# One core: the written order of a gated attention and ternary FFN kernel laid out anew, for all five engines

## The chip, the cores and the metric

The kernel runs on one core of a Trainium2 chip. The metric is the device time of one execution in microseconds (us). A core has a matmul engine (TensorE, here PE), VectorE (DVE), ScalarE (ACT), GpSimd (POOL) and SyncE (SP), which here only issues DMA transfers. SBUF is the on-chip working memory of 128 partitions, PSUM the memory that PE writes. About 1% of the time (14 us) is what a measurement of this kernel can tell from no change.

## The reference, cut to what matters

```python
def _L0_xattn_ref(q, k, v, Wq, Wk, Wv, Wo, bo, g):       # 8 heads of 64, DIM 128, b = 16, n = 1024
    qh = softmax(Wq q, over the 64 of a head) * 64 ** -0.5
    kh = softmax(Wk k, over n)
    vh = Wv v
    context = einsum('bhdn,bhen->bhde', kh, vh)
    out = einsum('bhde,bhdn->bhen', context, qh)
    out = Wo out + bo
    return out / norm(out over DIM) * g * sqrt(DIM)

def _bitlinear(x, w):
    scale = mean(abs(w))
    return x @ (round(clip(w / (scale + 1e-5), -1, 1)) * scale).T

x = x + tanh(g_xattn) * _L0_xattn_ref(layernorm(x), ctx, ctx, ...)      # x, ctx: (16, 128, 1024)
h = layernorm(x)
x = x + tanh(g_ffn) * _bitlinear(_bitlinear(h, w_gate) * _bitlinear(h, w_up), w_down)    # I = 2752
```

All values are float32 at the borders. Inside, the kernel splits most operands into a high and a low 16-bit part (`_hi`, `_lo`) and adds three products; ternary weights are kept as fp8.

## The kernel before, in words

The 16 batch elements go through the attention one by one (index i), and through the FFN in 8 groups of two (index g). Each piece of work is a *step* with a name and indices, and most steps take one to three instructions on one engine:

- Context side of i: `cabs`, `csum`, `cscale`, `c_hi`, `c_lo` scale and split the context rows; `kt(i,p)` (PE, L856) makes the keys of a pair of heads, `kmax` (DVE, L1496), `kexp` (ACT, L1224) the softmax; `kf_hi` (ACT), `kf_lo` (DVE, L1518, the subtraction L1358) split them; `turn_c`, `turn_k` are DMA transposes from SP; `ctxk` multiplies. `mprod`, `mev`, `mabs`, `msum`, `mscale`, `m_hi`, `m_lo` make the 128x512 matrix that the queries are multiplied with.
- Query side of i: `ln1` (DVE, L1491), `rstd1` and `q32` (POOL, L1756, L1769), `q_hi` (ACT), `q_lo` (POOL, L1776, the subtraction L1767); `qt(i,u)` (PE, L901), `qmax`, `qsub` (DVE, L1583, L1593), `qexp` (ACT, L1262), `qsum` (DVE, L1596, a reduce L1599 and a reciprocal L1601), `qnorm` (POOL, L1781), `qf_hi` (ACT), `qf_lo` (DVE, L1603, the operation L1361), `turn_q` (SP). For i = 0 and 1 the transposes are matmuls (`tr`, `ktr`, `zt`) in place of DMAs.
- Joining: `outp(i,hf)` (PE, L971), `yev` (ACT), `ss` (PE, L993), `ssg` (DVE, L1608), `rs` (POOL, L1787, the power L1790), `R` (PE, L1001), `x2m` (DVE, L1614), `x2a` (POOL, L1793), `ln2` (DVE), `rstd2` (POOL, L1762, the power L1764), `z` (DVE, L1635). Then z is split and transposed: by `zt` (PE, L878), `zt_hi` (ACT, L1170), `zt_lo` (DVE, L1646, L1358) for i = 0 and 1, by `z_hi`, `z_lo`, `turn_z` later.
- Weights: `wload` (SP) loads tiles of 128x1024 float32 into 13 slots; `wsum` (ACT and DVE) sums the absolute values; `wpart` (DVE, L1414), `wtotal` (PE, L964) and `wscale` (DVE, L1420) give the scale; the tiles are loaded once more, and `wquant` (POOL, L1745, the instruction L1754) and `wsign` (ACT, L1198, L1216) round them to fp8. Matrices 0 and 1 (gate and up) go first, matrix 2 (down) after them.
- FFN of group 0: `gu(0,j,s)` (PE, L1010, the matmul L1029), 22 chunks j of gate and up, then `gcopy` (ACT, L1327), `gmul` (DVE, L1704, the instruction L1709), `i_hi` (ACT, L1338), `i_lo` (DVE, L1713, the subtraction L1358 of 128x256), and `down(0,k,part)` (PE, L1080, L1113). The chunks use two PSUM banks in turn: `gu` of chunk j waits for `gmul` of j - 2. The first down product waits for `i_hi` and `i_lo` of chunks 0 to 20.
- FFN of groups 1 to 7: 20 of the 22 chunks are computed by seven products in place of eight. `form` (DVE and POOL, L1660 and L1813, 128x2048 fp8) makes sums and differences of the weights, `store_form` writes them to HBM, and for each group `load_form` (SP) brings them back; `product` (PE, L1042, the matmul L1064), `evict` (ACT, and DVE L1695), `pair_mul` (POOL, L1832), `pair_hi`, `pair_lo`, then `down` again.
- `reload`, `finish` (DVE, L1727) and `st_out` write the result.

Each engine runs its own instructions strictly in the order in which they are written. That order comes from one table, `WHEN`, which gives each step of each kind its place in one list of some 3,700 steps. `every_step()` names the steps, and each engine's `program` walks the list and emits the steps that it has. Between engines semaphores are waited for: a step that comes up before its input is there holds all that stands behind it on its engine.

```python
def program(steps):
    for _, kind, args in ORDER:
        if kind in steps:
            steps[kind](*args)
```

PSUM banks are handed on in the order in which the steps are written. `kt`, `qt`, `zt` and others share the pair PROJ (n even) and the pair TR (n odd, from i = 2 on): a PE step waits until the last user of the pair has been read, for `kt` by `kexp`, for `qt` by `qsub`, for `zt` by `zt_lo`. SP issues the DMAs of weights, transposes, forms and results, ACT those of x and the context.

Of the kernel before, what the change touches and what calls it, by code (L numbers as in the profile page):

```python
# [107 lines left out]
    "kexp": [27, 30, 99, 127, 169, 194, 209, 271, 357, 377, 399, 431, 468, 645, 648, 684, 768, 868, 922, 983, 1151, 1162,
        1199, 1222, 1248, 1346, 1355, 1377, 1422, 1547, 1558, 1571, 1760, 1767, 1800, 1827, 1941, 1965, 1982, 1989,
        2179, 2189, 2224, 2253, 2375, 2396, 2399, 2411, 2601, 2611, 2646, 2675, 2797, 2818, 2821, 2833, 3023, 3033,  # L110
        3068, 3097, 3214, 3228, 3239, 3249],
    "ktr": [66, 83, 112, 131, 187, 225, 261, 291],
    "k_f": [75, 87, 119, 135, 190, 231, 270, 296],
    "kf_hi": [365, 412, 445, 482, 531, 650, 693, 788, 851, 925, 989, 1017, 1158, 1192, 1228, 1251, 1285, 1350, 1374, 1403,
        1440, 1551, 1582, 1612, 1773, 1805, 1830, 1862, 1953, 1975, 1996, 2040, 2194, 2220, 2248, 2276, 2379, 2402,
        2419, 2462, 2616, 2642, 2670, 2698, 2801, 2824, 2841, 2884, 3038, 3064, 3092, 3120, 3218, 3237, 3252, 3304],
    "kf_lo": [374, 416, 451, 488, 541, 653, 725, 795, 858, 959, 994, 1025, 1163, 1198, 1233, 1255, 1308, 1354, 1378, 1409,
        1444, 1555, 1586, 1618, 1780, 1812, 1838, 1865, 1957, 1981, 2000, 2046, 2202, 2228, 2255, 2282, 2381, 2405,
        2425, 2468, 2624, 2650, 2677, 2704, 2803, 2827, 2847, 2890, 3046, 3072, 3099, 3126, 3220, 3240, 3256, 3320],
# [1758 lines left out]
```

## Time and profile before

| | us |
|---|---|
| median of 3 runs | 1412.72 |
| lowest and highest | 1410.63, 1420.97 |
| the profiled execution, its own time | 1418.48 |
| its span, first to last instruction | 1416.7 |
| PE busy | 1323.1 (93%) |
| VectorE busy | 1014.4 (72%) |
| ScalarE busy | 637.1 (45%) |
| GpSimd busy | 610.9 (43%) |
| mean granted TensorE clock | 0.97 |

Times in the rows count from the first instruction; the profiled execution is the span and 1.8 us around it. A row of busy times gives, for a stretch, each engine's busy microseconds with the number of instructions, the mean granted clock of TensorE (1 is full speed, 2.4 GHz), the DMA engines' share and rate. "A <- B" in a row of waits is what A's engine waited for.

### The profile page before, as it was taken

To read this page: it belongs to the slowest core of one execution; us is meant where nothing else is said; L and a number is where in the kernel's file an instruction comes from. 1 tells how busy PE (TensorE), PEld (TensorE's weight loads), DVE (VectorE), ACT (ScalarE), POOL (GpSimd) and SP (SyncE) were. 2 spreads that over 40 slices of the span, in tenths; PEclk is the share of its full clock that TensorE was granted. 3 is DMA by queue.
4 is the path that set the end of the run, shared out by engine and by line. 5 is a ranking of instruction groups with operands and counts; after the bars stand their busy time and mean duration, and the time that the engine had idled before them with its cause. 6 is when DMAs were issued, how large, how long until landed. Compare 5 with 4: busy or idle time off the path is not lost.

```text
span 1416.7 us, 31262 instructions
## 1 busy us (share of the span) xinstructions
PE 1323.1 (93%) x12888; PEld 970.6 (69%) x12888; DVE 1014.4 (72%) x1337; ACT 637.1 (45%) x866; POOL 610.9 (43%) x369
## 2 busy tenths in 40 slices
PE   4787698878989999999999999999999999999999
PEld 2554385663568955887578856987498757994994
DVE  6877499997878967687768785888568865842330
ACT  4677875554345444444434534454335433330220
POOL 0169755897533435354424460446234432231120
PEclk8898799999999999999999999999999999999999
DMA  9949998996898688778858896779767975664421
GB/s 358 408 152 332 287 268 258 248 226 154 209 206 203 157 172 181 166 180 177 207 129 182 179 193 150 182 176 202 186 155 175 191 168 124 166 154 111 137 79 45
DMA packets 410621, 270.30 MB, mean 191 GB/s; under 512 B 330032, under 2 KB 346800, under 8 KB 410480
## 3 DMA queue, kind: packets, MB, share of 16 engines
q1 hardware_dynamic: 403568, 243.13, 69.9%
q10 hardware_dynamic: 6912, 25.17, 5.7%
q8 instruction: 103, 1.69, 0.5%
q14 instruction: 38, 0.31, 0.1%
HBM read 161.55 MB, written 25.95 MB: 132 GB/s over the span
## 4 chain that ended last, share of the span: by engine, by line
PE 59%; DVE 1%; issue 0%; DMA 0%; POOL 0%; ACT 0%; SPq 0%; DVEq 0%; ACTq 0%; POOLq 0%
PE ps L1064 25%; PE ps L1113 16%; PE ps L817 5%; PE ps L818 5%; PE ps L819 5%; PE ps L1029 2%; PE ps L997 1%; PE ps L1005 1%; DMA kT<-k 0%; PE ps L834 0%; POOL q_raw L1773 0%; DVE k_unit L1474 0%; DVE w_gu L1695 0%; POOL w_gu L1832 0%; DVE q_stat L1599 0%
## 5 line engine op out<-in xcount | busy, mean ns | idle before, releaser
L1113 PE MATMUL ps<-w_dn,inter_buf 128*128 128x512 fp8e4 x1376 | 309.6, 380 | 4.4 <-ACT w_dn L1216 3.7
L1113 PEld LDWEIGHTS ps<-w_dn,inter_buf 128*128 128x128 f16 x1376 | 134.7, 99 | 160.4 <-ACT w_dn L1216 4.4
L1784 POOL TENSOR_TENSOR qs<-qs,q_stat 128x1024 f32<-128x1024 f32 x64 | 133.0, 2079 | 191.3 <-DVE q_stat L1601 190.7
L1064 PE MATMUL ps<-w_gu 128*128 128x128 f16 x3392 | 204.4, 219 | 3.1 <-issue 2.1
L1064 PEld LDWEIGHTS ps<-w_gu 128*128 128x128 fp8e4 x3392 | 195.3, 98 | 10.2 <-issue 3.9
L1832 POOL TENSOR_TENSOR w_gu<-w_gu 128x512 f32<-128x512 f32 x70 | 104.0, 1486 | 211.4 <-DVE w_gu L1695 147.3
L1064 PE MATMUL ps<-zT,w_gu 128*128 128x128 f16 x2528 | 155.3, 220 | 0.0
L1064 PEld LDWEIGHTS ps<-zT,w_gu 128*128 128x128 fp8e4 x2528 | 147.3, 99 | 6.0 <-issue 3.6
L1695 DVE SCALAR_TENSOR_TENSOR w_gu<-ps,w_gu 128x512 f32<-128x512 f32 x140 | 95.7, 684 | 73.9 <-PE ps L1064 72.8
L1029 PE MATMUL ps<-zT,w_gu 128*128 128x256 f16 x1024 | 119.2, 276 | 6.1 <-DVE gate L1709 6.1
L1029 PEld LDWEIGHTS ps<-zT,w_gu 128*128 128x128 fp8e4 x1024 | 101.5, 100 | 23.7 <-DVE gate L1709 7.2
L1500 DVE TENSOR_REDUCE kmx<-ps 128x1 f32<-128x1024 f32 x64 | 77.9, 1217 | 51.3 <-PE ps L819 39.3
L1790 POOL TENSOR_TENSOR rsv<-ssv,cst 128x4 f32<-128x4 f32 x32 | 42.5, 1329 | 157.3 <-DVE ssv L1612 157.3
L1125 ACT ACTIVATE w_gu<-ps 128x512 f32<-128x512 f32 x105 | 62.4, 595 | 99.2 <-PE ps L1064 99.2
L1583 DVE TENSOR_REDUCE q_stat<-ps 128x16 f32<-128x1024 f32 x64 | 77.9, 1218 | 33.4 <-PE ps L819 28.8
L1125 ACT ACTIVATE p<-qs 128x1024 f16<-128x1024 f32 x56 | 59.0, 1053 | 83.2 <-POOL qs L1784 53.0
L1361 DVE SCALAR_TENSOR_TENSOR p<-qs,p 128x1024 f16<-128x1024 f32 x56 | 79.6, 1421 | 18.4 <-ACT p L1125 18.3
L1230 ACT ACTIVATE ek<-ps,kbias,k_unit 128x1024 f32<-128x1024 f32 x56 | 67.3, 1201 | 56.0 <-DVE kbias L1509 55.7
L1268 ACT ACTIVATE qs<-qs,l_used 128x1024 f32<-128x1024 f32 x56 | 64.2, 1146 | 61.6 <-DVE qs L1593 52.9
L1125 ACT ACTIVATE inter_buf<-w_gu 128x512 f16<-128x512 f32 x70 | 43.8, 626 | 105.9 <-POOL w_gu L1832 105.7
L1797 POOL TENSOR_TENSOR xb<-xb,ysq 128x512 f32<-128x512 f32 x32 | 48.4, 1512 | 88.3 <-DVE ysq L1619 88.3
L1358 DVE TENSOR_TENSOR k<-ek,k 128x1024 f16<-128x1024 f32 x56 | 75.9, 1356 | 12.6 <-ACT k L1125 12.4
(192 smaller groups left out, 2660.3 us busy)
## 6 DMA issues: line engine op xcount, KB each, us to landing
w_gu<-forms SPq DMA_DIRECT2D x185, 256.0 KB, 3.1
ct_raw<-forms SPq DMA_DIRECT2D x60, 256.0 KB, 3.0
w_dn<-in_down_w SPq DMA_DIRECT2D x19, 512.0 KB, 5.0
xb<-in_x ACTq DMA_DIRECT2D x16, 512.0 KB, 6.0
x_dram<-xb SPq DMA_DIRECT2D x16, 512.0 KB, 4.1
fin<-x_dram SPq DMA_DIRECT2D x32, 256.0 KB, 2.8
out<-fin SPq DMA_DIRECT2D x32, 256.0 KB, 2.7
inter_buf<-in_up_w SPq DMA_DIRECT2D x15, 512.0 KB, 10.1
```

The lines of the kernel that those rows point to most:

```text
L817: nc.tensor.matmul(out_ap, a_h, b_h, start=start, stop=False)
L1029: last = nc.tensor.matmul(ps[:, rest_bank(g, j), s * T:s * T + T], w_gu[:, w, k, :], zT[:, h, k, :], start=(k == 0 and h == 0), stop=(k == ...
L1064: last = nc.tensor.matmul(o, form[:, c, k, :], moving(q, h, k), start=(fresh and c == 0 and k == 0 and h == 0), stop=(k == 3 and h == 1), ...
L1113: mm = nc.tensor.matmul(ps[:, down_bank(g, k), :], inter_of(g, j, u % 2, b), w_dn[:, j, hf * 512:hf * 512 + 512], start=(u == 0), stop=(u ...
L1125: return nc.scalar.activation(out_ap, in_ap, ACT.Copy, scale=scale)
L1358: return nc.vector.tensor_tensor(out_ap, a, b_ap, ALU.subtract)
L1361: return nc.vector.scalar_tensor_tensor(out=out_ap, in0=a, scalar=by, in1=b_ap, op0=ALU.mult, op1=ALU.subtract)
L1500: nc.vector.tensor_reduce(kmx[:, col], pair(proj_bank(i, p)), AX_X, ALU.max, negate=True).then_inc(k_maxed, 1)
L1583: nc.vector.tensor_reduce(q_stat[:, u % 2, 0, :], per_head(pair(proj_bank(i, u))), AX_X, ALU.max).then_inc(q_max, 1)
L1695: nc.vector.scalar_tensor_tensor(out=out, in0=ps[:, slot_bank(g, s, q), :], scalar=B_SCALE, in1=add, op0=ALU.mult, op1=ALU.add).then_inc(e ...
L1784: nc.gpsimd.tensor_tensor(v, v, q_stat[:, u % 2, 1, :].unsqueeze(2).broadcast_to([P, 2 * HEADS, DH]), ALU.mult).then_inc(q_prob, 1)
L1832: nc.gpsimd.tensor_tensor(v[:, :, 0, :], v[:, :, 0, :], v[:, :, 1, :], ALU.mult).then_inc(pair_muled, 1)
```

## The change

The table `WHEN` holds other places for the same steps. No step, instruction, wait, tile or transfer is added or taken away, and `every_step`, `program` and the steps' own code are the same; only the order within each engine's list changes. By engine: SP has 635 steps of which 232 stand at another place, by 11 places at most; PE 924, 478, 30; ACT 775, 455, 24; DVE 1023, 626, 39; POOL 363, 165, 7. The diff, cut (the numbers are places in the one list; the k-th number of a kind belongs to its k-th step):

```diff
@@ -89,244 +89,244 @@
...
 WHEN = {
...
-    "qnorm": [96, 134, 148, 186, 265, 311, 338, 367, 516, 533, 563, 623, 680, 798, 830, 928, 957, 1018, 1048, 1072, 1136,
...
+    "qnorm": [96, 134, 148, 186, 271, 313, 366, 377, 495, 522, 588, 631, 709, 795, 833, 950, 977, 1022, 1047, 1074, 1147,
...
-    "rs": [200, 273, 385, 433, 704, 850, 979, 1035, 1145, 1227, 1425, 1468, 1573, 1630, 1761, 1810, 1961, 2012, 2183,
...
+    "rs": [200, 267, 404, 436, 718, 849, 984, 1037, 1163, 1232, 1419, 1470, 1579, 1654, 1751, 1812, 1951, 2012, 2176,
...
-    "x2a": [211, 297, 398, 441, 737, 877, 992, 1050, 1180, 1252, 1435, 1475, 1598, 1649, 1779, 1832, 1983, 2039, 2197,
...
+    "x2a": [211, 290, 414, 444, 734, 884, 1000, 1053, 1181, 1250, 1427, 1481, 1605, 1662, 1777, 1835, 1970, 2039, 2193,
...
-    "rstd2": [318, 453, 912, 1060, 1268, 1483, 1658, 1849, 2070, 2305, 2492, 2727, 2914, 3148, 3302, 3494],
+    "rstd2": [310, 455, 909, 1063, 1261, 1491, 1678, 1888, 2070, 2300, 2492, 2722, 2914, 3144, 3302, 3494],
-    "zt": [362, 471],
+    "zt": [379, 486],
-    "zt_lo": [371, 477],
+    "zt_lo": [387, 505],
-    "ln1": [22, 48, 210, 491, 665, 956, 1089, 1329, 1525, 1728, 1963, 2154, 2330, 2576, 2752, 2998],
+    "ln1": [22, 50, 210, 494, 678, 957, 1090, 1307, 1506, 1750, 1975, 2154, 2392, 2576, 2814, 2998],
-    "qt": [74, 79, 106, 155, 213, 220, 282, 324, 479, 483, 539, 592, 651, 718, 773, 874, 926, 997, 1016, 1049, 1095,
-        1181, 1257, 1263, 1310, 1434, 1462, 1487, 1577, 1632, 1673, 1698, 1808, 1844, 1882, 1930, 2015, 2048, 2083,
...
+    "qt": [74, 79, 106, 155, 213, 220, 327, 338, 474, 476, 539, 583, 662, 713, 785, 906, 932, 997, 1020, 1052, 1089,
+        1179, 1251, 1260, 1321, 1434, 1454, 1480, 1546, 1614, 1677, 1704, 1820, 1843, 1865, 1922, 2014, 2048, 2083,
...
-    "qsum": [91, 128, 143, 182, 235, 305, 325, 358, 509, 528, 558, 619, 671, 791, 820, 923, 950, 1013, 1043, 1067, 1132,
...
+    "qsum": [91, 128, 143, 182, 235, 289, 358, 368, 490, 517, 579, 627, 694, 788, 824, 945, 973, 1018, 1041, 1070, 1142,
...
-    "gu": [487, 493, 500, 506, 513, 521, 527, 534, 542, 549, 562, 571, 576, 582, 596, 609, 617, 624, 638, 644, 647,
...
+    "gu": [509, 514, 523, 528, 533, 545, 552, 559, 564, 569, 592, 596, 603, 608, 617, 629, 641, 648, 671, 675, 677,
...
-    "i_lo": [520, 536, 548, 561, 573, 597, 612, 631, 681, 714, 716, 747, 782, 789, 824, 826, 846, 865, 879, 917, 929,
-        941, 1140, 1153, 1565, 1584, 2006, 2014, 2428, 2436, 2850, 2858, 3267, 3274, 3550, 3556],
+    "i_lo": [531, 553, 565, 582, 600, 635, 645, 649, 665, 720, 722, 755, 781, 798, 829, 832, 855, 859, 887, 899, 933,
+        934, 1137, 1141, 1564, 1589, 1997, 2015, 2416, 2440, 2838, 2862, 3257, 3275, 3550, 3556],
-    "form": [277, 568, 575, 588, 649, 687, 691, 708, 740, 775, 784, 819, 810, 839, 866, 884, 871, 967, 982, 995],
+    "form": [283, 566, 573, 595, 618, 669, 674, 681, 736, 766, 775, 818, 817, 864, 874, 890, 935, 982, 989, 1005],
-    "wtotal": [219, 224, 712],
+    "wtotal": [219, 224, 705],
-    "wscale": [223, 228, 717],
+    "wscale": [223, 228, 716],
-    "wquant": [227, 232, 237, 241, 246, 250, 253, 257, 260, 279, 283, 289, 293, 303, 307, 321, 326, 329, 334, 342, 347,
-        352, 356, 360, 364, 373, 376, 381, 390, 394, 401, 403, 406, 411, 417, 422, 426, 430, 436, 450, 455, 461,
...
+    "wquant": [227, 232, 237, 241, 246, 250, 253, 259, 262, 280, 286, 294, 299, 303, 307, 321, 324, 328, 332, 337, 342,
+        344, 349, 354, 359, 363, 373, 382, 385, 389, 392, 397, 399, 406, 410, 420, 425, 428, 432, 447, 451, 458,
...
-    "turn_c": [314, 565, 870, 1099, 1294, 1449, 1726, 1899, 2143, 2363, 2565, 2785, 2987, 3203],
+    "turn_c": [316, 585, 854, 1099, 1294, 1463, 1656, 1874, 2144, 2355, 2566, 2777, 2988, 3199],
-    "turn_k": [380, 420, 460, 492, 564, 659, 731, 801, 872, 966, 999, 1030, 1167, 1204, 1237, 1262, 1314, 1359, 1385, 1415,
...
+    "turn_k": [370, 419, 460, 491, 584, 658, 729, 805, 856, 920, 980, 1003, 1158, 1201, 1239, 1269, 1302, 1380, 1414, 1438,
...
```

Read out of the table, the stretches of the engines' lists that are spoken of below (last index 0 left out, a span of tiles written once):

```
POOL before: qnorm(1,1) rstd2(0) wquant x4 qnorm(1,2) wquant x6 qnorm(1,3) wquant x3 rs(1,0) wquant x2 x2a(1,0)
             wquant x8 rs(1,1) wquant(0,19) x2a(1,1) wquant(1,19) rstd2(1) wquant x4 q_lo(2)
POOL after:  qnorm(1,1) wquant x11 qnorm(1,2) wquant(0,13) qnorm(1,3) wquant x6 rs(1,0) wquant x2 x2a(1,0)
             wquant x4 rs(1,1) x2a(1,1) wquant(1,19) wquant(0,20) rstd2(1) wquant x3 q_lo(2)
PE before:   kt(3,0) zt(1) qt(2,0) qt(2,1) gu(0,0,0) gu(0,0,1)
PE after:    kt(3,0) qt(2,0) qt(2,1) zt(1) kt(3,1) gu(0,0,0) gu(0,0,1)
DVE before:  z(1) kmax(3,0) wsum(2,0) zt_lo(1) qmax(2,0) kf_lo(2,3) ln1(3) qsub(2,0) qmax(2,1) gmul(0,0)
             qsum(2,0) qsub(2,1) i_lo(0,0) gmul(0,1)
DVE after:   z(1) kmax(3,0) wsum(2,0) qmax(2,0) qsub(2,0) qmax(2,1) kf_lo(2,3) qsum(2,0) ln1(3) qsub(2,1)
             zt_lo(1) qf_lo(2,0) qsum(2,1) cabs(4) gmul(0,0) kf_lo(3,0) i_lo(0,0) wsum(2,3) wsum(2,6) gmul(0,1)
POOL before: rstd1(4) q32(4) qnorm(3,0) form(1,2) rs(2,0) form(1,5) wquant(2,0)
POOL after:  form(1,2) form(1,5) rstd1(4) q32(4) qnorm(3,0) rs(2,0) wquant(2,0)
DVE before:  gmul(0,10) qf_lo(2,3) i_lo(0,9) i_lo(0,10) wscale(2)
DVE after:   gmul(0,10) wscale(2) i_lo(0,9) i_lo(0,10)
DVE before:  gmul(0,18) form(4,4) i_lo(0,18) cc_lo(3) qmax(3,3) ln2(2) qf_lo(3,2) qsub(3,3) gmul(0,19) gmul(0,20)
             kmax(4,2) mev(3) i_lo(0,19) mabs(3) qsum(3,3) mscale(3) i_lo(0,20)
DVE after:   gmul(0,18) kmax(4,1) qf_lo(3,2) i_lo(0,18) gmul(0,19) ln2(2) mev(3) i_lo(0,19) mabs(3) gmul(0,20)
             gmul(0,21) kf_lo(4,1) qmax(3,3) kmax(4,2) z(2) qsub(3,3) i_lo(0,20) i_lo(0,21) form(4,4)
```

## Rows read from the trace of the kernel before

**Rows 1.** Busy time of each engine by stretch: us, busy, (instructions), clock, DMA.
```profile
0.00:75.00 75.00, 48.03 (x160) 29.95 (x161) 57.15 (x85) 40.59 (x67) 7.17 (x12) 0.82 0.99 385
75.00:180.00 105.00, 78.19 (x341) 49.03 (x340) 69.39 (x98) 83.83 (x98) 81.23 (x63) 0.85 0.79 252
180.00:323.00 143.00, 118.36 (x898) 90.73 (x895) 139.36 (x152) 86.15 (x135) 103.27 (x46) 0.94 0.95 252
323.00:450.00 127.00, 116.77 (x982) 77.32 (x983) 97.43 (x126) 54.88 (x69) 60.57 (x35) 0.96 0.86 187
450.00:1417.00 967.00, 961.78 (x10516) 723.59 (x10513) 651.12 (x880) 371.66 (x499) 358.63 (x215) 1.00 0.70 160
```

**Rows 2.** PE's waits from 450 on: total, times, longest.
```profile
PE ps L1064 <- DVE w_gu L1695: 0.9, 2, 0.5
```

**Rows 3.** PE's waits from 180 to 323.
```profile
PE ps L817 <- DVE qs L1593: 6.2, 2, 3.6
```

**Rows 4.** DVE by group and shape, 180 to 330: busy, mean ns, idle.
```profile
L1358 DVE TENSOR_TENSOR inter_buf<-gate,inter_buf 128x256 f16<-128x256 f32 x21 | 28.5, 1366 | 0.0
L1361 DVE SCALAR_TENSOR_TENSOR p<-qs,p 128x1024 f16<-128x1024 f32 x7 | 14.3, 2046 | 0.8 <-ACT p L1125 0.8
...
L1667 DVE TENSOR_TENSOR ct_raw<-w_gu 128x2048 fp8e4<-128x2048 fp8e4 x4 | 10.2, 2544 | 0.0
...
L1709 DVE SCALAR_TENSOR_TENSOR gate<-ps,gate 128x256 f32<-128x256 f32 x21 | 8.5, 411 | 0.1
```

**Rows 5.** Timeline 203.5 to 209, all engines: start, us, instruction, [idle before].
```profile
203.70 3.95 POOL L1818 TENSOR_TENSOR w_gu<-w_gu 128x2048 fp8e4<-128x2048 fp8e4 x1 [2.23 <-DVE w_gu L1672]
...
204.48 1.20 DVE L1411 TENSOR_REDUCE absum<-w_dn 128x1 f32<-128x1024 f32 x1
...
205.60 3.13 DVE L1361 SCALAR_TENSOR_TENSOR p<-qs,p 128x1024 f16<-128x1024 f32 x1
```

**Rows 6.** Timeline of POOL, 80 to 170.
```profile
117.84 1.90 POOL L1784 TENSOR_TENSOR qs<-qs,q_stat 128x1024 f32<-128x1024 f32 x1 [1.44 <-DVE q_stat L1601]
...
139.61 1.01 POOL L1790 TENSOR_TENSOR rsv<-ssv,cst 128x4 f32<-128x4 f32 x1
...
156.37 1.01 POOL L1790 TENSOR_TENSOR rsv<-ssv,cst 128x4 f32<-128x4 f32 x1
...
159.43 1.26 POOL L1797 TENSOR_TENSOR xb<-xb,ysq 128x512 f32<-128x512 f32 x1 [0.94 <-DVE ysq L1619]
...
162.53 1.47 POOL L1764 TENSOR_TENSOR mv<-mv,cst 128x1 f32<-128x1 f32 x1 [0.74 <-DVE mv L1489]
...
167.93 2.13 POOL L1767 TENSOR_TENSOR qn<-q_raw,qn 128x1024 f16<-128x1024 f32 x1
```

**Rows 7.** Timeline of DVE, 160 to 182.
```profile
171.53 1.22 DVE L1358 TENSOR_TENSOR zT<-ps,zT 128x1024 f16<-128x1024 f32 x1 [2.87 <-ACT zT L1125]
175.66 1.23 DVE L1583 TENSOR_REDUCE q_stat<-ps 128x16 f32<-128x1024 f32 x1 [2.90 <-PE ps L819]
```

**Rows 8.** Timeline of PE, 140 to 182.
```profile
146.50 5.37 PE L985 MATMUL ps<-eT,m 128*128 128x512 f32 x8 [1.11 <-ACT eT L1125]
...
168.50 1.07 PE L884 MATMUL ps<-ident,ysq 128*128 128x128 f32 x8 [3.54 <-ACT ek L1230]
172.90 0.58 PE L817 MATMUL ps<-wq,qn 128*128 128x512 f16 x1 [3.33 <-DVE zT L1358]
...
177.59 4.64 PE L1029 MATMUL ps<-zT,w_gu 128*128 128x256 f16 x41
```

**Rows 9.** Timeline of POOL, 218 to 260.
```profile
234.01 1.00 POOL L1760 TENSOR_TENSOR mv<-mv,cst 128x1 f32<-128x1 f32 x1 [13.86 <-DVE mv L1489]
...
254.02 4.34 POOL L1754 TENSOR_SCALAR w_dn<-w_dn,wthr 128x1024 f32<-128x1024 f32 x3 [1.25 <-DVE wthr L1429]
```

**Rows 10.** PE's waits from 323 to 450.
```profile
PE ps L1113 <- ACT w_dn L1216: 3.7, 3, 2.7
PE ps L1005 <- issue: 3.3, 1, 3.3
```

More of the change, by code:

```diff
@@ L108 @@
[L108 to L119, printed above, removed]
@@ new lines @@
+    "kexp": [27, 29, 99, 127, 169, 194, 209, 273, 322, 380, 405, 437, 471, 570, 654, 679, 767, 882, 929, 974, 1139, 1152,
+        1187, 1224, 1247, 1355, 1365, 1400, 1426, 1528, 1537, 1576, 1733, 1782, 1795, 1808, 1946, 1962, 1965, 1998,
+        2180, 2187, 2218, 2249, 2375, 2382, 2400, 2421, 2602, 2609, 2640, 2671, 2797, 2804, 2822, 2843, 3024, 3031,
+        3062, 3093, 3217, 3224, 3239, 3258],
+    "ktr": [66, 83, 112, 131, 187, 225, 265, 281],
+    "k_f": [75, 87, 119, 135, 190, 231, 270, 298],
@@ new lines @@
+    "mabs": [636, 903, 1088, 1371, 1519, 1687, 1901, 2102, 2328, 2524, 2750, 2946, 3172, 3373],
+    "msum": [639, 937, 1092, 1376, 1534, 1690, 1908, 2108, 2333, 2530, 2755, 2952, 3177, 3375],
+    "mscale": [78, 107, 640, 949, 1103, 1381, 1542, 1699, 1911, 2112, 2338, 2534, 2760, 2956, 3182, 3378],
+    "m_hi": [643, 951, 1110, 1384, 1549, 1702, 1912, 2123, 2344, 2545, 2766, 2967, 3188, 3383],
+    "m_lo": [647, 954, 1113, 1388, 1553, 1709, 1917, 2126, 2348, 2548, 2770, 2970, 3192, 3386],
+    "ld_xq": [1, 163, 473, 622, 928, 1064, 1278, 1492, 1722, 1944, 2138, 2362, 2560, 2784, 2982],
[3 rows of a table added]
@@ new lines @@
+    "q_hi": [467, 594, 915, 1055, 1267, 1483, 1710, 1928, 2125, 2352, 2547, 2774, 2969, 3196],
+    "q_lo": [469, 607, 921, 1058, 1270, 1486, 1714, 1935, 2129, 2353, 2551, 2775, 2973, 3197],
[4 rows of a table added]
+    "qmax": [81, 103, 113, 165, 221, 249, 333, 346, 479, 485, 548, 593, 672, 732, 794, 919, 952, 1002, 1025, 1056, 1106,
+        1188, 1259, 1272, 1325, 1437, 1460, 1484, 1555, 1620, 1695, 1718, 1823, 1860, 1871, 1937, 2019, 2054, 2088,
+        2132, 2236, 2265, 2282, 2354, 2437, 2476, 2510, 2554, 2658, 2687, 2704, 2776, 2859, 2898, 2932, 2976, 3080,
+        3109, 3126, 3198, 3282, 3332, 3343, 3407],
@@ new lines @@
+    "tr": [102, 146, 193, 206, 314, 334, 384, 396],
+    "e_f": [109, 151, 197, 215, 319, 339, 391, 402],
+    "qf_hi": [503, 567, 626, 706, 761, 827, 877, 985, 1007, 1040, 1069, 1166, 1204, 1234, 1304, 1429, 1445, 1473, 1497,
+        1600, 1629, 1660, 1729, 1766, 1846, 1885, 1923, 1971, 2032, 2085, 2133, 2191, 2263, 2298, 2321, 2398, 2454,
+        2507, 2555, 2613, 2685, 2720, 2743, 2820, 2876, 2929, 2977, 3035, 3107, 3142, 3165, 3233, 3299, 3348, 3374,
+        3431],
+    "qf_lo": [508, 571, 630, 708, 773, 836, 881, 987, 1012, 1046, 1080, 1169, 1211, 1236, 1313, 1430, 1449, 1475, 1500,
+        1604, 1637, 1663, 1738, 1771, 1850, 1897, 1930, 1973, 2038, 2089, 2143, 2197, 2268, 2305, 2326, 2401, 2460,
+        2511, 2565, 2619, 2690, 2727, 2748, 2823, 2882, 2933, 2987, 3041, 3112, 3149, 3170, 3238, 3307, 3354, 3380,
```

197 lines of the change are left out of this document (91 added, 106 removed), and 166 rows, old and new, of the table WHEN.

## The prediction

> **What bounds the kernel now.** I read the busy times by stretch first [rows 1]. TensorE (PE) is busy 1323.1 of 1416.7 us, so it stands idle for 93.6 us, and nearly all of that lies early: 27.0 us before 75, 26.8 us from 75 to 180, 24.6 us from 180 to 323 (the time at which the first down product begins), 10.2 us from 323 to 450. From 450 to 1416.7 it is idle for 5 us of 967, most of it after the last matmul; its largest wait there comes to 0.9 us in two pieces [rows 2]. The change leaves the number of matmuls alone. So what it can bring lies in the idle 88.6 us before 450, and after 450 it can only lose.
>
> The second reading is what fills the stretch 180 to 323: VectorE (DVE) is busy 139.4 of 143 us there [rows 1], and PE's largest wait names it (6.2 us for L1593's subtraction, which gives a bank back) [rows 3]. DVE is the bound of that stretch. It isn't all work. The `i_lo` subtraction of 128x256 takes 1366 ns on average, 21 times, while its neighbour L1709 of the same size takes 411 [rows 4]. One overlap shows how: a `qf_lo` (L1361, 128x1024) starts at 205.60, while GpSimd (POOL) is in a `form` from 203.70 to 207.65, and takes 3.13 us; the same operation has a mean of 2046 ns in this stretch. A reduce of as many elements that starts 1.1 us earlier, under the same POOL instruction, takes its usual 1.20 [rows 5]. DVE operations with two inputs in SBUF are held until POOL's instruction is over. The excess is 21 x (1.37 - 0.41) = 20 us on `i_lo` and 7 x (2.05 - 1.2) = 6 us on `qf_lo`, 26 us of 139.
>
> **The change part by part.** Nothing is added or removed; each engine gets its own instructions in another order, and SP its DMA issues. I walk the places where the order moves something past the chain that feeds PE, in time.
>
> (1) 0 to 75: only neighbours among the small scale steps change places. Cost 0.
>
> (2) POOL from 88 to 170. The chain to the first `gu` goes through POOL's queue: rs(1,1) at 156.37, x2a(1,1) at 159.43, rstd2(1) at 162.53, and q_lo(2) from 167.93 to 170.06, with `wquant` tiles between [rows 6]. Waits of 0.94 and 0.74 us stand there, because x2a and rstd2 come up in the queue before DVE has delivered. The new list has the same steps ahead of q_lo(2). rs(1,1) has one `wquant` more ahead, x2a(1,1) none more, rstd2 one more. So POOL does its tile before it needs DVE and the wait of 0.74 goes; an earlier wait of 1.44 us of qnorm(1,1) for DVE's row sums [rows 6] should go too, as qsum(1,1) moves ahead of qsub(1,2). Against it stands that x2a(1,1) now follows rs(1,1) with no tile between: its wait grows from 0.94 to about 2. Net -1 to -2; I take -1.5. Bounds: 0 and -4 (all of POOL's waits there), and on the other side +3 (a rival below).
>
> (3) The start of `gu`. Before, zt(1) stands ahead of qt(2,0) on PE. DVE waits 2.87 us for ScalarE's (ACT) copy, does zt_lo, and waits 2.90 us for qt(2,0) [rows 7]; PE runs zt(1) at 168.50, qt(2,0) from 172.90 and `gu` from 177.59 [rows 8]. In the new order qt(2,0) and qt(2,1) go first, then zt(1), then kt(3,1), then `gu`. qt(2,0) needs bank PROJ back from kexp(3,0), on which zt(1) waited 3.54 us until 168.50 before, and q_lo(2), which ends at 168.6 after (2): about 168.6. At the slow pace of rows 8 (2.35 us each) it ends at 171; qmax to 172.2, qsub to 173.4, zt(1) to 174.5. On DVE qmax(2,1), kf_lo(2,3), qsum(2,0), ln1(3) and qsub(2,1) now precede zt_lo(1): four steps of 1.2 to 1.4 us and the statistics, some 1.6, together 6.7. So zt_lo(1) ends near 181.3. kt(3,1) needs bank TR back from the same qsub(2,1). So `gu` starts at about 181.5 to 182, 4 us later than now. But in that time DVE has done seven steps that stood behind zt_lo before, and its idle time falls from 5.8 us to some 2.2 (168.7 to about 171). As DVE bounds what follows, its 3.6 us count, not PE's 4: the late `gu` is covered by PE's own 24.6 us of idle time up to 323. Term: -3.6. If PE rather than DVE turns out to be the bound there, this reads +4; those are its ends.
>
> (4) DVE up to i_lo(0,20), the last one that the first down product waits for. Behind it now: a qsum (1.2 and a small reciprocal), form(4,4) (2.5 by the mean of L1667) [rows 4], three one-column instructions of mscale; 4.4 together. Ahead of it now: z(2) (some 0.8), kf_lo(4,1) (1.2), gmul(0,21) (0.4), 2.4. Term: -2.0. The lock excess I leave at its 26 us: both engines keep their work in the stretch. Ends: -13, half of it gone, and 0 for the whole term.
>
> (5) The down weights. wscale(2) stood behind two `i_lo`, which are now behind it (2 x 1.37), and wtotal(2) behind a `gu` on PE: 4 us sooner together. POOL can use them: form(1,2) and form(1,5) move ahead of rstd1(4), into a hole in which POOL waits 13.86 us for DVE's row statistics. So `wquant` of the down weights should start about 4 us before 254.02 [rows 9], and end some 6 us sooner, since a qnorm of 2 us is no longer ahead of the last tile. PE comes to the down product 7.1 us sooner by (2) to (4), so its wait of 3.7 us for the down weights [rows 10] grows by 1.1. Ends: 0 and +3.7.
>
> (6) SP's queue: turn_k(3,0) and turn_c(3) go behind six more weight loads, turn_k(4,3) goes ahead of eight form loads. All of it lies under PE work that doesn't wait in the trace; 0. As ends I take -3 and +3, since a gap of 3.3 us at L1005 [rows 10] has no releaser that the profile names, and can go or come again.
>
> (7) After 450: 0. With 33% of DVE's time and 63% of POOL's free [rows 1] the cushions stand. A gain is excluded, as PE has no idle time there to give.
>
> Sum: -1.5 - 3.6 - 2.0 + 1.1 = -6.0 us. The profiled execution took 1418.5 (span 1416.7 and 1.8 around it), so 1412.5 for it; its own time lies 5.8 above the median of the runs, 1412.7, and the same six microseconds off that give 1406.7.
>
> The overlap of [rows 5] bears on a rule of the Trainium skill, "SBUF — State Buffer", section "Who interferes with whom": a VectorE instruction with two SBUF inputs and a GpSimd instruction that reads SBUF exclude each other for the whole instruction, and whoever starts first holds the ports. The trace agrees (3.13 us against about 1.2). By that rule the locked time of both engines adds up in whatever order they stand, and an order can only choose who waits; it speaks against a large gain.
>
> **The rivals.** A: the new order fits the holding up. If half of the 26 us excess in 180 to 323 goes, DVE reaches i_lo(0,20) 13 us sooner still: 1406.7 - 13 = 1394, less what the down weights then hold back, say 1395. For it: the bound engine carries the excess. Against it: POOL is busy 103 of the 143 us, and almost the same forms, tiles and qnorms stay in the stretch, so a DVE step finds POOL inside an instruction about as often.
>
> B: slower by POOL's queue. qnorm(1,2) has seven `wquant` more ahead, rs(1,0) five. rs(1,0) ended at 140.6 [rows 6]; a tile takes 1.1 (x2a(1,1) ends at 160.69, rstd2's wait begins at 161.79), so five make that 146.1, and outp(1,1), which stands behind R(1,0) on PE, started at 146.50 [rows 8]. The cushion is just used up. If the tiles are held by DVE, as the three of rows 9 (4.34, 1.45 each), it is 147.9, and all of batch 1's tail comes 2 to 3 us later: term (2) reads +3; and if PE then has no room for the late `gu`, term (3) reads +4. With (4) and (5) that is +6: 1419. It decides from the point at which R(1,0) runs after 147.5.
>
> C: slower by a steady stall. Each of the groups 1 to 7 gets a new order as well. If in the six groups from 450 on one DVE or POOL step comes 2.5 us late for a product, that costs 15 less the six: 1422 to 1428. The waits of rows 2 speak against it, and PE's idle time there would have to grow threefold.
>
> D: nothing moves: gains in DVE's queue are eaten by PE's order and by rows that come a little later. 1413.
>
> **How the numbers follow.** Forecast .37, A .20, D .18, B .15, C .10. Likeliest 1407; its own range by the ends of the terms is 1399 to 1415. The range reaches down to A and up past B: 1393 to 1422. About 1% (14 us) is what a measurement of this kernel tells from no change: faster by more than that needs A or a good part of it, .22; slower needs C or a bad B, .13; .65 within.
>
> **What would show it.** PE idle from 75 to 450 down from 61.6 to about 55; `gu` starting at 181 to 182 after zt(1) and kt(3,1), with DVE idle under 3 us between 167 and 182; the first down matmul at 316 to 317; down `wquant` starting near 250; `i_lo` still at 1.2 to 1.4 us in the stretch; from 450 on the same 962 us of PE work and no wait above 1 us. I am wrong if `i_lo` falls under 0.9 (A), if R(1,0) runs after 147.5 or DVE is idle over 8 us from 180 to 320 (B), or if PE waits more than 5 us in total after 450 (C).

## The result, and the profile after

| | before | after |
|---|---|---|
| median of the runs beside which the change was first timed | 1415.7 us (4 runs) | 1399.4 us (4 runs, 1397.8 to 1401.5) |
| the same, timed again with more runs (the last experiment) | 1411.8 us (11 runs) | 1400.2 us (6 runs, 1398.4 to 1405.0) |
| profiled execution (span) | 1418.48 (1416.7) | 1401.51 (1399.7) |

The ratio is 0.9886, with a 95% interval from 0.9841 to 0.9930, in the first set and 0.9921 (0.9896 to 0.9946) in the second. The change makes the kernel about 12 us faster by the second set, some 0.8%. That is less than the 14 us which a single measurement can tell, but both intervals lie below 1. The forecast was 1407 and the range 1393 to 1422.

The busy times by stretch of the kernel after, in the columns of [rows 1]:

```profile
0.00:75.00 75.00, 48.20 (x160) 29.38 (x160) 56.80 (x85) 40.32 (x67) 7.17 (x12) 0.82 1.00 385
75.00:180.00 105.00, 72.19 (x318) 44.63 (x316) 72.28 (x100) 85.14 (x99) 82.29 (x63) 0.89 0.78 251
180.00:323.00 143.00, 124.88 (x950) 94.63 (x951) 129.09 (x159) 91.94 (x142) 104.57 (x49) 0.95 0.99 263
323.00:450.00 127.00, 123.16 (x1200) 89.75 (x1197) 102.62 (x134) 55.48 (x72) 64.56 (x36) 0.97 0.87 199
450.00:1399.00 949.00, 946.37 (x10268) 708.89 (x10265) 637.15 (x863) 362.34 (x489) 339.85 (x211) 1.00 0.68 160
```

Two things stand out. From 75 to 180 PE is busy 6 us less than in [rows 1]: fewer matmuls fall into the stretch (318 against 341, as `gu` starts only after 180), and the granted clock is higher (0.89 against 0.85). From 180 to 323 DVE is busy 129.1 us where it was 139.4, and PE 124.9 where it was 118.4. After 450 PE's largest waits of [rows 2] are gone: the view of its waits has no row left.

DVE by group and shape, 180 to 330, of the kernel after; these answer to [rows 4]:

```profile
L1358 DVE TENSOR_TENSOR inter_buf<-gate,inter_buf 128x256 f16<-128x256 f32 x21 | 20.6, 993 | 2.3 <-ACT inter_buf L1125 2.2
...
L1361 DVE SCALAR_TENSOR_TENSOR p<-qs,p 128x1024 f16<-128x1024 f32 x7 | 9.7, 1392 | 0.2 <-ACT p L1125 0.2
...
L1667 DVE TENSOR_TENSOR ct_raw<-w_gu 128x2048 fp8e4<-128x2048 fp8e4 x4 | 9.4, 2339 | 0.0
...
L1709 DVE SCALAR_TENSOR_TENSOR gate<-ps,gate 128x256 f32<-128x256 f32 x21 | 8.6, 416 | 4.8 <-ACT gate L1125 4.8
```

`i_lo` (L1358) takes 993 ns instead of 1366 and `qf_lo` (L1361) 1392 instead of 2046: 8 and 4.6 us less. These are the two operations whose holding behind GpSimd the prediction had counted. DVE also has idle time again: 4.8 us at L1709, and from 180 to 320 13.9 us in all, where it was 3.5 before. So it no longer bounds the stretch alone. PE's waits there, 180 to 323, answer to [rows 3]:

```profile
PE ps L817 <- ACT ek L1230: 7.2, 2, 6.4
PE ps L1029 <- DVE gate L1709: 5.7, 4, 4.2
PE ps L817 <- DVE qs L1593: 5.2, 1, 5.2
PE ps L834 <- DVE mmx L1365: 2.2, 1, 2.2
```

DVE's subtraction gave way to ScalarE's exponent as the largest. And from 323 to 450, where [rows 10] had 3.7 us for the down weights, one wait is left:

```profile
PE ps L1064 <- issue: 3.7, 1, 3.7
```

PE's timeline around the start of `gu` answers to [rows 8]: the row product R(1,0) at 145.81, then qt(2,0), zt(1), kt(3,1), `gu`, and at 315.12 the first down matmul, which came at 323.25 before:

```profile
145.81 0.65 PE L1005 MATMUL ps<-ident,rsv 128*128 128x128 f32 x4 [3.36 <-POOL rsv L1790]
...
169.66 0.59 PE L817 MATMUL ps<-wq,qn 128*128 128x512 f16 x1 [6.97 <-POOL qn L1767]
...
175.04 1.06 PE L884 MATMUL ps<-ident,ysq 128*128 128x128 f32 x8 [0.53 <-DVE qs L1593]
...
181.36 0.61 PE L817 MATMUL ps<-c,wk 128*128 128x512 f16 x1 [5.25 <-DVE qs L1593]
...
183.89 2.29 PE L1029 MATMUL ps<-zT,w_gu 128*128 128x256 f16 x18
...
315.12 7.28 PE L1113 MATMUL ps<-w_dn,inter_buf 128*128 128x512 fp8e4 x28
```

### The profile page after: what moved, and what is told of

Read it like the earlier page. It is cut to its first block, busy times and chain, and to the rows that moved or that the text cites. A ratio compares the mean times of both kernels' runs of the same rounds, so it can differ in the third digit from the quotient of the medians.

```text
span 1399.7 us, 31262 instructions
## 1 busy us (share of the span) xinstructions
PE 1314.8 (94%) x12888; PEld 967.3 (69%) x12888; DVE 997.9 (71%) x1337; ACT 635.2 (45%) x866; POOL 598.5 (43%) x369
## 4 chain that ended last, share of the span: by engine, by line
PE 81%; POOL 9%; issue 4%; DVE 4%; SPq 1%; DMA 1%; POOLq 0%; ACT 0%; ACTq 0%; DVEq 0%
PE ps L1064 31%; PE ps L1113 21%; PE ps L817 7%; PE ps L818 7%; PE ps L819 7%; PE ps L1029 4%; POOL w_dn L1754 3%; PE ps L997 2%; POOL stage_c L1754 1%; POOL inter_buf L1754 1%; PE ps L1005 1%; POOL w_gu L1818 1%; DVE absum L1411 1%; POOL fin L1754 1%; PE ps L870 1%
## 5 line engine op out<-in xcount | busy, mean ns | idle before, releaser
L1113 PE MATMUL ps<-w_dn,inter_buf 128*128 128x512 fp8e4 x1376 | 307.9, 380 | 0.0
L1113 PEld LDWEIGHTS ps<-w_dn,inter_buf 128*128 128x128 f16 x1376 | 135.1, 99 | 155.0 <-issue 1.1
L1500 DVE TENSOR_REDUCE kmx<-ps 128x1 f32<-128x1024 f32 x64 | 77.6, 1212 | 33.2 <-PE ps L819 21.9
L1268 ACT ACTIVATE qs<-qs,l_used 128x1024 f32<-128x1024 f32 x56 | 64.1, 1144 | 76.8 <-DVE qs L1593 76.3
L1790 POOL TENSOR_TENSOR rsv<-ssv,cst 128x4 f32<-128x4 f32 x32 | 38.6, 1207 | 129.2 <-DVE ssv L1612 129.2
L1599 DVE TENSOR_REDUCE q_stat<-qs 128x16 f32<-128x1024 f32 x64 | 77.7, 1214 | 17.1 <-ACT qs L1268 17.0
L1358 DVE TENSOR_TENSOR k<-ek,k 128x1024 f16<-128x1024 f32 x56 | 81.4, 1453 | 10.0 <-ACT k L1125 10.0
L1361 DVE SCALAR_TENSOR_TENSOR p<-qs,p 128x1024 f16<-128x1024 f32 x56 | 81.7, 1459 | 4.4 <-ACT p L1125 4.2
```

The source lines that it names most:

```text
L1113: mm = nc.tensor.matmul(ps[:, down_bank(g, k), :], inter_of(g, j, u % 2, b), w_dn[:, j, hf * 512:hf * 512 + 512], start=(u == 0), stop=(u ...
L1361: return nc.vector.scalar_tensor_tensor(out=out_ap, in0=a, scalar=by, in1=b_ap, op0=ALU.mult, op1=ALU.subtract)
```

## The experiments

The first reading offers three causes, the holding (theory H), the order alone (O) and the scale of the down weights (D), and leaves open in which part of the program the gain is made. Five of the kernels here (e1 to e4, e9) are spliced: all steps up to a named one in one order, and every step that is left in the other. Every kernel here but e5 and e12 has a table that is three lines longer, so a line number in its trace is 3 higher (L1116 for L1113). As code a splice is a change of the table alone; here are two rows of it, and of each kernel only the rule is told below:

```diff
     "zt": [362, 471],
-    "wscale": [223, 228, 717],
+    "wscale": [223, 228, 716],
-    "turn_zs": [1113, 1116, 1521, ...
+    "turn_zs": [1114, 1121, 1539, ...
```

(e1: zt as in before, wscale and turn_zs as in after.)

**Where the gain is made.** Four splices.

e1, before up to gu(0,0), then after:

> The order of before up to the first gate/up matmul gu(0,0), every remaining step in the order of after. Theory by stage (the gain was made behind gu(0,0), the prologue of after only cost 6.3 us): gu(0,0) starts at 177 to 178 as in before, first down matmul at 309 to 312, end 5 to 7 us ahead of after, 1392 to 1395. Rival (after's later gu(0,0) is work paid in advance: zt, kt(3,1), a row block further on): gu(0,0) at 177 to 178, first down at 314 to 318, end within 3 us of after, 1397 to 1402. Rival (the order after gu(0,0) does nothing, clocks and luck of the prologue do): 1410 or more.

e2, after's order only between gu(0,0) and the first down matmul, before's ahead of it and behind it:

> The order of before, with after's order only for the steps between gu(0,0) and the first down matmul. If the stage of the gate/up matmuls makes the gain alone: first down matmul at 309 to 312 instead of 323, down(0,2) 345 to 350, end 12 to 15 us below before, 1400 to 1404. If the gain also needs the steady groups' order: 3 to 4 us less, 1404 to 1408. If it needs the order of the prologue: within 5 us of before.

e3, before up to the first down matmul, then after:

> The order of before up to the first down matmul, then that of after. If the steady groups' order counts for nothing and the down stage only profited from earlier down weights: first down matmul at 323, end within 2 us of before, 1413 to 1417. If the order behind down(0,0) has its own part of the gain (5.6 us to down(0,2), 3.3 us in the rest): 1406 to 1411.

e4, the mirror, after up to the first down matmul, then before:

> The order of after up to the first down matmul, then that of before; the mirror of the run before. If the order behind down(0,0) counts for nothing: first down at 315, end within 2 us of after, 1398 to 1402. If it has its own part: 1404 to 1409.

| | median us | ratio to before (95%) |
|---|---|---|
| e1 | 1404.9 | 0.9946 (0.9926 to 0.9966) |
| e2 | 1409.2 | 0.9991 (0.9968 to 1.0014) |
| e3 | 1408.4 | 0.9968 (0.9953 to 0.9983) |
| e4 | 1406.0 | 0.9952 (0.9935 to 0.9968) |

None of the theories of one place holds. e3 and e4 came out as forecast for an order behind down(0,0) that has a part of its own, and share the change out between them: 0.32% behind the first down matmul, 0.48% up to it, 0.80% together, and the whole measures 0.79% (the last experiment). e1 missed all three of its forecasts: gu(0,0) started at 186.95, since the splice puts the work that either order has ahead of gu(0,0) ahead of it, and the first down matmul came at 318.1. From gu(0,0) on e1 and after run alike: 131.2 us each to the first down matmul. In e2 the first down matmul came at 318.0, not at 309 to 312. e2's median is not told from before; seven of its 12 runs lie at 1407.0 to 1409.2 and five at 1414.9 to 1422.9, with none between. What that is comes below.

**Was the first profile of before an ordinary one?** e5 is the kernel before, unchanged.

> The kernel before, unchanged, for a second profile, since its first profiled execution (1418.48 us) lies above most of its runs. If that execution was ordinary: waits of 6 us between 392 and 418 us again, product(1,2,0) at 444 to 445. If it caught an interruption of its own: 3 to 6 us less there, 1412 to 1414 in all, every step before 390 us within 1 us of its old place.

It took 1413.01 us. Of the steps compared up to product(1,0,0), at 397 us, all but kt(3,0) (1.3 us earlier) lie within 0.4 us of their old places (first down matmul 323.54 against 323.25); the way from there to product(1,1,0) then takes 19.1 us instead of 26.1. So the first profile, on which the prediction's sum stands, held an interruption of its own. It has two places. At 413.4 PE stops inside R(4,0), between the third and the fourth of its four matmuls, where the program has no wait:

```profile
416.72 0.37 PE L1005 MATMUL ps<-ident,rsv 128*128 128x128 f32 x1 [3.34 <-issue]
```

Between 413.8 and 416.6 no engine is busy, and behind it PE runs 2.8 us at half clock. What stopped them the profile doesn't show; in e5 the four matmuls follow each other. The other place is the two transposes turn_zs on the sync queue, on which product(1,0,1) waits; in four profiles it starts 0.09 us after the second has landed. First the profile of before (landed at 404.36), then e5 (402.48), 1.9 us of the 7.0:

```profile
393.30 8.95 SPq L755 DMA_TRANSPOSE w_gu<-w_gu  x2
```

```profile
392.87 7.50 SPq L755 DMA_TRANSPOSE w_gu<-w_gu  x2
```

Measured against e5, the change is worth 11.5 us by its first profile (1401.51) and 14.5 by its second (1398.48); the medians of the larger set give 11.6.

With this I cut every trace at the same steps and sum, for PE, the time it was idle, the busy time at half clock (the granted clock at the lower of its two levels, 1.2 GHz), and the work in time at full clock, which is the busy time less half of the time at half clock. Up to the first down matmul the same steps are done in all of them:

| up to the first down matmul | us | idle | at half clock | work |
|---|---|---|---|---|
| before (e5) | 323.5 | 79.3 | 59.9 | 214.4 |
| e2: order of after from gu(0,0) on | 318.0 | 77.3 | 53.2 | 214.1 |
| e4: order of after | 317.0 | 75.5 | 56.2 | 213.4 |
| after | 315.1 | 77.6 | 47.0 | 213.8 |
| after again (e12) | 315.8 | 78.5 | 46.0 | 214.1 |

So the order of after brings 6.3 to 8.4 us up to here (e11 below has its first down matmul at 317.2), and PE's idle time, the only thing that the prediction had looked at, falls by 0.8 to 3.8. Most of the rest is time at half clock, which goes from 60 us to 46 to 56 and counts half: 6.5 to 7 us in the two profiles of after, but only some 1.8 in e4 and e11, where the idle time is the larger part. That the idle time hardly changes is the sum of two shifts, which a cut at gu(0,0) takes apart:

| | to gu(0,0): us, idle, half clock | from there to the first down matmul |
|---|---|---|
| before (e5) | 177.9, 54.3, 43.2 | 145.6, 24.9, 16.6 |
| e1: order of after from gu(0,0) on | 186.9, 60.8, 46.4 | 131.2, 16.8, 6.4 |
| e4: order of after | 183.1, 59.6, 42.1 | 133.9, 15.8, 14.1 |
| after | 183.9, 61.0, 40.5 | 131.2, 16.8, 6.5 |

In the stage of the gate and up matmuls the order of after saves 14.4 us: 8.1 of idle time, 5.0 by the clock, 1.3 of work. Ahead of it, it costs 6.0, since steps of DVE and kt(3,1), which before has in the stage, now stand in front of it. The late `gu` isn't free: with one order the stage takes the same time wherever it starts (131.2 us from 183.9, 184.5, 186.8 and 186.9; 145.6 to 145.7 from 176.6, 177.9 and 178.3 in e3, e5 and e9), so the first down matmul comes later by as much as `gu` does.

Behind the first down matmul, the three columns one after the other:

| | first down matmul to down(0,2) | from there to product(1,2,0) | from there to the end of PE's work |
|---|---|---|---|
| order of before: e5, e2, e4 | 39.0, 39.7, 39.9 | 75.4, 75.4, 75.7 | 969.9, 969.1, 968.5 |
| order of before, first profile | 38.9 | 82.4 | 968.7 |
| order of after: after, e1, e3 | 33.4, 33.3, 34.0 | 82.3, 82.0, 83.8 | 965.5, 966.3, 965.9 |
| order of after: e12 | 33.4 | 77.8 | 966.4 |

Here the order of after gains some 5.6 us in the down stage and 2 to 4 in the steady groups, and loses 2.4 to 8.4 between (1.3 of it is work moved ahead out of the groups). The gains in the down stage are the waits for w_dn, 3.7 us, and 3 us less at half clock.

**The holding.** e6 and e7 are before and after with GpSimd's row work of that stretch cut down; they leave those rows unfinished and serve for their times alone.

```diff
-                    nc.gpsimd.tensor_tensor(form_place(s, 2), form_place(s, 1), form_base(s, 0, 0),
+                    w = 64 if s < 2 else 512
+                    nc.gpsimd.tensor_tensor(form_place(s, 2)[:, :, :, 0:w], form_place(s, 1)[:, :, :, 0:w], form_base(s, 0, 0)[:, :, :, 0:w],
...
+                w = 128 if i in (3, 4) else N
+                nc.gpsimd.tensor_scalar(q_raw[:, 0:w], q_raw[:, 0:w], mv[:, 0:1], mv[:, 3:4], ALU.subtract,
...
+                w = DH // 8 if i == 2 or (i, u) == (3, 0) else DH
```

> The order of before; GpSimd's row work between 165 and 320 us is cut to an eighth of its columns: qnorm of block 2 and qnorm(3,0), q32(3), q32(4), q_lo(3), form(0,2), form(0,5), form(1,2), form(1,5), so those rows are left unfinished. Theory H (VectorE held up behind GpSimd is what the order of after avoids): VectorE's excess over its shortest forms falls from 43 us to 15 or less here and the stage from gu(0,0) to the first down matmul from 145.7 us to 128 to 135. Rival O (the order of the steps alone, not the hold): the excess falls as well, but the stage stays at 139 to 146.

> The order of after with the same columns of GpSimd's row work left out. Theory H: the stage from gu(0,0) to the first down matmul goes from 131.2 to 125 to 130 us, and the two light kernels differ in it by 0 to 5 us, where the whole ones differ by 14.4. Rival O: the two light kernels still differ by 10 us or more in this stage.

e6: 1405.4 us, ratio 0.9938 (0.9918 to 0.9958). e7: 1392.2 us, 0.9843 (0.9810 to 0.9877). `i_lo` in e6 and in e7, in the view of [rows 4]:

```profile
L1361 DVE TENSOR_TENSOR inter_buf<-gate,inter_buf 128x256 f16<-128x256 f32 x21 | 13.8, 662 | 0.2 <-ACT inter_buf L1128 0.2
```

```profile
L1361 DVE TENSOR_TENSOR inter_buf<-gate,inter_buf 128x256 f16<-128x256 f32 x21 | 16.1, 776 | 0.1
```

In e6 `i_lo` takes less than half of its time in before, and less than in either form of after. DVE's whole excess between gu(0,0) and the first down matmul (each instruction against the shortest of its line and shape in these profiles) is 39 us in before, 23 in e6, 22 in after and 18 in e7. The expectation's count, 43 for before, includes some 4 us more, and its 15 or less was not reached. Yet the first down matmul comes at 319.0 in e6 and 310.6 in e7: 8.5 us apart, where the whole kernels are 7.8 to 8.4 apart. The stage from gu(0,0) differs by 11.9 us (139.7 and 127.9) against 14.4. Theory H wanted 0 to 5, O 10 or more; only e7's own stage lies where H had it. So 16 us less holding bought at most 5.9 us of stage in e6, a third of its size. At most, since the cut makes GpSimd's own queue shorter too: in e7 the same cut brings the first down matmul 4.6 us forward, as much as in e6 (4.5), with only 4 us less holding. The lead of after doesn't rest on the holding: it stays where the two are 5 us apart in it. Up to the first down matmul the lead is the clock again: 60.4 us at half clock in e6, 43.9 in e7, with 75.3 and 76.3 us idle.

**The down weights' scale.** e8 and e10 move single steps in the order of before. In e10, on PE and on DVE:

```diff
 DVE: i_lo(0,8) ... wpart(2) ... gmul(0,10) qf_lo(2,3)
+     wscale(2)
      i_lo(0,9) i_lo(0,10)
-     wscale(2)
 PE:
+     wtotal(2)
      gu(0,11,0) ...
-     wtotal(2)
```

e8 adds, on POOL:

```diff
+     form(1,2) form(1,5)
      rstd1(4) q32(4) qnorm(3,0)
-     form(1,2)
      rs(2,0)
-     form(1,5)
      wquant(2,0)
```

> The order of before with three small moves towards that of after: wtotal(2) on TensorE right behind wpart(2), wscale(2) on VectorE ahead of i_lo(0,9), form(1,2) and form(1,5) on GpSimd ahead of rstd1(4). Theory D (the down weights' scale and GpSimd's turn are a good part of the gain): quantising of the down weights starts at 246 to 250 instead of 254, TensorE's waits for w_dn of 3.7 and 0.7 us go, the end is 4 to 6 us earlier, 1406.5 to 1408.5. Rival H (only the fit of VectorE's and GpSimd's row work counts): quantising starts 1 to 4 us earlier, the first down matmul stays at 322 to 324, the end within 2 us of before.

> The order of before with two moves: wtotal(2) on TensorE right behind wpart(2), and wscale(2) on VectorE ahead of i_lo(0,9) instead of behind i_lo(0,10); GpSimd's queue is as before. Theory D in its small form (the two i_lo ahead of the scale hold the down weights back): from qt(2,0) to the first quantising of a down weight 3 to 5 us less than the 81.1 us of before, the waits for w_dn in the down stage (3.7 us) 2 to 4 us shorter, the end 2 to 4 us earlier, 1408.5 to 1410.5. Rival (GpSimd sets when the quantising starts): it starts within 1 us of before, the end too.

e8: 1417.7 us, 1.0020 (0.9997 to 1.0044). The first down matmul came at 332.2, and the quantising at 263.8 instead of 254.3: rs(2,0) now stands behind two forms on POOL, and PE ran R(2,0) 9.9 us later than in e5. But 5.6 of this were lost before any moved step, by gu(0,0) at 183.5. This run refutes the moves of `form` in before's surroundings (3.1 us worse from gu(0,0) to product(1,2,0)) and can say no more. e10: 1410.9, 0.9986 (0.9965 to 1.0007). The scale was ready 4.6 us sooner, the quantising started 1.6 us sooner, the first down matmul came 0.9 sooner, and the waits for w_dn stood at 3.5 us. GpSimd's queue sets the start (its `form` ends only at 252.8, and the first tile follows); of theory D 0.9 us is seen at the first down matmul, and the end isn't told from before.

That the wait of the down stage hangs on something else is seen in e2, whose quantising starts at 250.0, and which still has it; PE's waits of e2, 318 to 450:

```profile
PE ps L1116 <- ACT w_dn L1219: 3.3, 2, 2.6
```

while e3, whose quantising starts at 253.0, has none; its waits from 323 on:

```profile
PE ps L1067 <- issue: 5.3, 1, 5.3
PE ps L820 <- issue: 0.8, 1, 0.8
```

e3 differs from e5, and e4 from after, in the order behind the first down matmul alone: the wait goes from 3.7 us to none in the one pair and from none to 3.2 in the other. The old order puts qnorm(3,3) and qnorm(4,0) on GpSimd ahead of the last tiles, and its last wsign ends at 340.5 in e5; the new one has one qnorm there and runs kt(4,3) on PE before down(0,0,4), and ctxk(4,0) before the last part of down(0,0), and there the last wsign ends at 322.8 in after and 334.1 in e3. Counted from the first down matmul it ends 17.0 us later in e5, e2 and e4, 11.9 in e3 and 7.7 in after.

**The prologue alone.** e9, after up to qt(2,0), then before.

> The order of after up to qt(2,0), the last step of TensorE's prologue that both orders place alike, then that of before. If the prologue has a part of its own in the gain (qt(2,0) at 169.7 instead of 173.2): qt(2,0) at 169 to 170 and the end 2 to 4 us below before, 1408.5 to 1411. If the gain is made only behind it: within 1 us of before. If the order of after ahead of gu(0,0) is a cost, as the first reading of the trace has it: 1414 or more.

1411.9 us, 0.9993 (0.9976 to 1.0010): not told from before. qt(2,0) came at 173.8, not at 169 to 170, since zt(1) goes ahead of it in the old order, and the first down matmul at 323.9. Up to there PE was idle 82.4 us and at half clock 55.2: what its prologue saved in clock it waited. The new prologue counts only with the stage behind it (e1, without it, has its first down matmul 2.4 to 3.0 us behind after).

**The wait that came, and after once more.** e11 takes after and moves three steps:

```diff
 SP:
-     st_out(0,3)
      turn_zs(1,1) turn_zs(1,0)
+     st_out(0,3)
 PE:  kt(5,1)
+     csum(6,0) ss(4,0)
      product(1,0,1) product(1,0,2)
-     csum(6,0) ss(4,0)
```

> The order of after with the store st_out(0,3) moved on the sync queue behind the two transposes turn_zs(1,1) and turn_zs(1,0), and csum(6,0) and ss(4,0) on TensorE ahead of product(1,0,1), as before has them. If the wait of 3.7 us ahead of product(1,0,1) in after is the wait for these transposes: it shrinks to 0 to 1.5 us and the end is 2 to 4 us below after, 1395.5 to 1397.5. If it is another transfer's: it stays at 3 us or more, and the end within 1 us of after.

> The kernel after, unchanged, against many runs of before, and for a second profile. If its first profile was lucky in the clock (13.4 us at half clock between qt(2,0) and the first down matmul, where two other runs with the same order there had 20.5): 17 to 21 us at half clock there, first down matmul at 316.5 to 317.5, own time 1403 to 1404, ratio to before 0.992 to 0.994. If the clock follows from the order: 13 to 14 us at half clock, 315 us, 1399 to 1401.5, ratio 0.989 to 0.991.

e11: 1402.5 us, 0.9925 (0.9902 to 0.9949); e12: 1400.2 us, 0.9921 (0.9896 to 0.9946). In e11 the wait of 3.7 us is gone, waits of 1.5 and 0.5 us are left, and the stretch from down(0,2) to product(1,2,0) takes 78.4 us instead of 82.3. But e12, with nothing moved, has

```profile
PE ps L1064 <- issue: 1.6, 1, 1.6
```

and 77.8 us. The wait differs between executions of one kernel by as much as e11 was to save, so e11's profile shows nothing for its moves, and its median is not below that of after. No kernel here that does the whole work beats after. e12's forecast about the clock came out on the second side: 13.4 us at half clock between qt(2,0) and the first down matmul, as in the first profile, where e4 and e11, with the same order of steps there, have 20.5 and 20.6; its ratio fell to the edge of the first. So two profiles of after agree, and yet the order of these steps alone doesn't fix the clock.

## Why the prediction was right, and where its steps were not

The sign held and the time lies within the range, but that is in good part luck. The measured 1399.4 and 1400.2 lie nearer to rival A (1395) than to the forecast (1407); of some 12 us gained the sum has 6, and most of its terms did not come as told. Step by step:

- **(1), 0 to 75:** as said, 48.2 us busy against 48.0.
- **(2), POOL's queue, -1.5:** not seen. R(1,0) came 2.9 us later (145.8, still ahead of the 147.5 of rival B), q_lo(2) ended 0.5 us sooner (169.6 for 170.1) instead of 1.5, the waits did not go but moved, to 2.53 us at rs(1,1) and 1.57 at x2a(1,1), and e9 is not told from before with the prologue alone.
- **(3), start of `gu`, -3.6:** the order on PE came as told, but at 183.9, not 181.5 to 182: qt(2,0) ran 1.1 us later than told, and kt(3,1), which the sum leaves out, took 2.5 us at half clock behind qsub(2,1). DVE's idle time stayed at 5.4 us (3.33 ahead of a qmax at 172.4, 2.10 ahead of a gmul at 188.2) instead of 2.2. That the late `gu` costs nothing failed: PE's idle time ahead of it grew by 6.7 us, and with one order the first down matmul comes as much later as `gu` does. What DVE did in that time made the stage behind shorter; the runs show only the sum of both, 6.0 us lost and 14.4 gained.
- **(4), DVE up to i_lo(0,20), -2.0 with the excess left at 26 us:** this step failed. The excess of the two operations fell from 26 to about 13.5 us, which was rival A's mechanism. Rival A's price failed too: it made 13 us of it at the first down matmul, where e6 shows at most a third of the holding's size, and e6 against e7 that after's lead stands without it. DVE turned much of what it gained into idle time (13.9 us from 180 to 320 for 3.5).
- **(5), the down weights, +1.1:** the sign was wrong. Quantising started 7.2 us sooner and its last tile came 17.7 us sooner than in e5 (told: 4 and 6), with PE 8.4 us sooner. So the whole wait of 3.7 us went, and with it 1.5 us of slow clock: 5.6 us in the down stage. I had looked at when the quantising starts; e2, e3 and e10 show that the last tiles decide, and what stands ahead of them and of the matmuls that need them.
- **(6), SP, 0 within -3 and +3:** the gap of 3.3 us at L1005 belonged to the one execution. In after the wait for turn_zs is 1.6 to 3.7 us, and the way from down(0,2) to product(1,2,0) takes 2.4 to 6.9 us longer than in e5, of which 1.3 is work from later groups.
- **(7), after 450, 0 and no gain possible:** 2 to 4 us were gained behind product(1,2,0), 1 to 2.6 of them idle time, and 1.3 is work done earlier.
- **Left out:** the clock. The sum had no term for it, though [rows 1] show 0.85 and 0.94 in two stretches. At half clock PE spent 60 us up to the first down matmul before, and 46 to 47 in both profiles of after, which is 6.5 to 7 us; summed up to there it is the largest single term in them.
- **The base:** the sum starts from an execution that held 7.0 us of its own; only the step back to the median kept the forecast from that.
- **The signs:** PE's idle time from 75 to 450 came to 54.8 us as told (55), but from a base that held the interruption: e5 has 57.3, not 61.6. DVE's idle time from 180 to 320 was a sign of rival B if over 8 us; it was 13.9, though the kernel is faster and R(1,0) ran in time. So that sign can't tell B from a DVE with less to do. `i_lo` at 0.99 us lies between the 1.2 of the forecast and the 0.9 of rival A.
- **The range:** the ends that the terms are given don't add up to 1399 to 1415; from the median they make 1389 to 1426.

On the rule of the Trainium skill, "SBUF — State Buffer", section "Who interferes with whom": its lock is seen again, as 1366 ns against 662 in e6, where GpSimd's instructions are short. What I drew from it, that an order can only choose who waits, isn't what it states, and the runs are against it: with the same instructions on both engines, DVE's excess in the stage went from 39 us to 22, and GpSimd's fell as well, from 20.8 to 18.8. An order can also bring together instructions that don't hold each other, as the reduce of [rows 5], which took its usual 1.20 us beside GpSimd.

What stays open: why the order of after gives fewer stretches at half clock. The clock of e4 and e11 shows that the order of the steps doesn't fix it. And of the 6.3 to 8.4 us up to the first down matmul I can't say which of the moved steps make them: e1, without after's prologue, has 5.4 of them, and after's prologue adds 2.4 to 3.0 only when the stage behind it is there too.

## What to carry to other kernels

An engine that is busy all through a stage, with a quarter of it spent being held, doesn't have to be worth that quarter: price a hold by what the engine behind it waits for, and test it by cutting the work of the holder in both kernels. When TensorE is idle in many short pieces, sum its idle time and its time at half clock between equal steps, at more than one cut: here idle time nearly the same in sum was 8 us less in one stage and 7 us more ahead of it. Take a second profile of the kernel before ahead of any sum made against it. Cut a reordered program by splices at a step that both orders reach with the same work done: the shares of e3 and e4 add up to the whole, those of e1 and e9 (0.54% and 0.07%) come to less, if within their intervals.
